# Turned blocks of probabilities and blocks of the values product, one after the other within a slot

## The reference, cut to what matters

```python
s = jnp.einsum('bhqd,bhkd->bhqk', q, k) * scale
s = jnp.where(mask[None, None], s, jnp.finfo(s.dtype).min)
p = jax.nn.softmax(s, axis=-1)
return jnp.einsum('bhqk,bhkd->bhqd', p, v)
...
attn = _causal_attn(q, k, v, SCALE)
lat = _causal_attn(q, lk, lv, SCALE)
return attn @ w_o + lat @ w_lo
```

## Time and profile before

| | us |
|---|---|
| median of 3 runs | 1983.04 (1981.39 to 1983.26) |
| profiled execution | 1982.13 |
| its span, first to last instruction | 1979.6 |
| TensorE busy | 1949.8 (98%) |
| VectorE busy | 1348.5 (68%) |
| GpSimd busy | 1128.6 (57%) |
| ScalarE busy | 1032.7 (52%) |

### The profile page before, as it was taken

How to read it: one execution, slowest core, us unless ns; L and a number is a source line. 1 busy time by engine, 2 the same in 40 slices (tenths; PEclk the granted TensorE clock), 3 DMA queues, 4 the chain that set the end, 5 groups by cost and what they waited for, 6 DMA issues and landing times.

```text
span 1979.6 us, 30315 instructions
## 1 busy us (share of the span) xinstructions
PE 1949.8 (98%) x11104; PEld 1727.1 (87%) x11104; DVE 1348.5 (68%) x3242; ACT 1032.7 (52%) x2335; POOL 1128.6 (57%) x904
## 2 busy tenths in 40 slices
PE   7999999999999999999999999999999999999997
PEld 5989889898898988989898898988989888898985
DVE  5757757576675857757487584766757577575766
ACT  3654627456273653727447273563726547274564
POOL 4647566474754756556475564756546565564750
PEclk8999999999999999999999999999999999999999
DMA  7030120302103030030400203021040300303001
GB/s 265 1 129 3 40 102 12 120 1 101 41 12 120 1 126 16 12 120 1 142 0 27 105 1 141 1 89 43 1 141 1 118 14 18 125 2 116 1 12 43
DMA packets 53074, 117.03 MB, mean 59 GB/s; under 512 B 6848, under 2 KB 8896, under 8 KB 52800
## 3 DMA queue, kind: packets, MB, share of 16 engines
q10 hardware_dynamic: 33936, 69.21, 9.6%
q1 hardware_dynamic: 18992, 45.90, 7.0%
HBM read 108.81 MB, written 6.29 MB: 58 GB/s over the span
## 4 chain that ended last, share of the span: by engine, by line
PE 96%; ACT 2%; DVE 1%; ACTq 1%; POOL 0%; issue 0%; DMA 0%; SPq 0%
PE ps L438 28%; PE ps L440 27%; PE ps L439 27%; PE ps L526 13%; ACT probs L719 1%; ACTq L749 0%; DVE probs L974 0%; ACT acc L794 0%; PE ps L641 0%; PE ps L626 0%; POOL pt_lo L875 0%; ACT k_hi L685 0%; ACT val_hi L685 0%; DMA acc<-xT 0%; DVE stats L1042 0%
## 5 line engine op out<-in xcount | busy, mean ns | idle before, releaser
L903 POOL TENSOR_TENSOR probs<-probs,inv_sum 128x640 f32<-128x640 f32 (+7 forms) x512 | 584.4, 1147 | 383.8 <-DVE inv_sum L981 383.7
L974 DVE CUSTOM_DVE_ANT_0 probs<-ps,mask 128x640 f32<-128x640 f32 (+7 forms) x512 | 383.5, 751 | 68.8 <-PE ps L440 63.4
L719 ACT ACTIVATE probs<-probs,neg_max 128x640 f32<-128x640 f32 (+7 forms) x512 | 398.0, 778 | 52.6 <-DVE neg_max L974 47.5
L915 DVE TENSOR_TENSOR pt_lo<-ps,pt_hi 128x512 fp32r<-128x512 f32 (+3 forms) x512 | 269.2, 549 | 156.5 <-ACT pt_hi L685 156.5
L526 PE MATMUL ps<-ident,probs 128*128 128x128 f32 x2304 | 335.7, 273 | 0.0
L685 ACT ACTIVATE pt_hi<-ps 128x512 fp32r<-128x512 f32 (+3 forms) x512 | 234.3, 489 | 184.2 <-PE ps L526 184.2
L685 ACT ACTIVATE ql_hi<-probs 128x512 fp32r<-128x512 f32 x128 | 81.0, 633 | 439.1 <-POOL probs L894 439.1
L526 PEld LDWEIGHTS ps<-ident,probs 128*128 128x128 f32 x2304 | 274.5, 140 | 27.4
L894 POOL TENSOR_TENSOR probs<-probs 128x512 f32<-128x512 f32 x144 | 186.4, 1295 | 167.6 <-DVE probs L951 167.5
L438 PE MATMUL ps<-val_hi,ql_hi 128*128 128x512 f32 x512 | 205.6, 401 | 0.0
L875 POOL TENSOR_TENSOR pt_lo<-raw,pt_hi 128x1024 fp32r<-128x1024 f32 (+1 forms) x47 | 94.3, 2021 | 191.3 <-ACT pt_hi L685 191.3
(11 more groups left out here) (109 smaller groups left out, 4435.7 us busy)
## 6 DMA issues: line engine op xcount, KB each, us to landing
x_hi<-x_kept ACTq DMA_DIRECT2D x30, 1024.0 KB, 8.8
x_lo<-x_kept ACTq DMA_DIRECT2D x30, 1024.0 KB, 12.2
raw<-wo SPq DMA_DIRECT2D x32, 512.0 KB, 3.6
raw<-wq SPq DMA_DIRECT2D x16, 512.0 KB, 3.9
raw<-wlv SPq DMA_DIRECT2D x16, 512.0 KB, 4.5
raw<-wkv SPq DMA_DIRECT2D x8, 512.0 KB, 7.5
acc<-xT SPq DMA_DIRECT2D x4, 512.0 KB, 6.0
wlk_raw<-wlk SPq DMA_DIRECT2D x16, 128.0 KB, 3.4
```

The costliest lines, as they stand in the source:

```text
L719: nc.scalar.activation(dst, dst, ACT.Exp, bias=neg_max[:, n % 8:n % 8 + 1], scale=-1.0, accum_out=row_sum[:, n % 8:n % 8 + 1]).then_inc(q[ ...
L903: nc.gpsimd.tensor_tensor(b, b, inv_sum[:, k % 8:k % 8 + 1].to_broadcast([P, b.shape[-1]]), ALU.mult).then_inc(q["normed"], 1)
L915: return nc.vector.tensor_tensor(dst, src, h, ALU.subtract)
L974: nc.vector.tensor_tensor_reduce(out=probs_of(n).rearrange("p (b n) -> p b n", b=b), in0=scores_of(n), in1=mask[:, S - w:S].rearrange("p ( ...
```

## The change

In a slot in which a tile is turned and pieces of `PV_AFTER` stand, the pieces are handed to `turn_probs`. It issues one piece (three matmuls, one j) behind each turned block until none is left; pieces that remain follow behind the last block. The signals, the waits and the matmuls themselves are the same, at other places of TensorE's order. The other engines' programs are unchanged.

```diff
-            def turn_probs(g, pair, n):
+            def turn_probs(g, pair, n, between):
+
                 pe.wait_ge(q["normed"], per_pair(g, pair, TILES, n + 1))
...
                     for b in range(b0, b1):
                         mm = pe.transpose(ps[:, T_BANKS[u % len(T_BANKS)], P * (b - b0):P * (b - b0) + P],
                                           probs_of(n)[:, P * b:P * b + P], ident[:])
-                    mm.then_inc(q["turned"], 1)
+                        if b == b1 - 1:
+                            mm.then_inc(q["turned"], 1)
+                        if between:
+                            with_values(g, pair, *between.pop(0))
+                for piece in between:
+                    with_values(g, pair, *piece)
...
+                        pieces = [(m, j, j + 1) for m, j0, j1 in PV_AFTER.get(k, ()) for j in range(j0, j1)]
                         if 0 <= k - T_LAG < TILES:
-                            turn_probs(g, pair, k - T_LAG)
-                        for m, j0, j1 in PV_AFTER.get(k, ()):
-                            with_values(g, pair, m, j0, j1)
+                            turn_probs(g, pair, k - T_LAG, pieces)
+                        else:
+                            for piece in pieces:
+                                with_values(g, pair, *piece)
```

## The result

| | before | after |
|---|---|---|
| median of 6 runs, us | 1982.83 (1981.39 to 1983.90) | 1988.97 (1988.52 to 1991.02) |
| profiled execution, its span | 1982.13, 1979.6 | 1988.90, 1986.2 |

The ratio is 1.0033 with the interval 1.0021 to 1.0045: the change costs 6.1 us. The forecast was 9.6 us, or 1992.6 us in all.

A forecast was written before the change was run, and what follows sets the result against it. TensorE's own list of work was taken to bound the kernel. Extra runs of blocks, 1.9 us, plus the wait of scores(28), 7.7, made 9.6; 1983.04 + 9.6 = 1992.6 us, own range 1989 to 1995 (chance 0.70), wide range 1985 to 1999.

The forecast's parts named there:

- What bounds the kernel: TensorE's own list of work sets the time; hardly a wait to remove, 1.3 us in 8 times on `neg_max`.
- (a): Eight reordered slots: 15 more runs of turned blocks per pair, 0.008 us each over 16 pairs, 1.9 us lost.
- (b): Slot 24's later blocks delay ScalarE and VectorE; new TensorE wait at scores(28), 0.48 us in each of 16 pairs, 7.7 us.
- The sign that was named for it: TensorE's list of waits: `neg_max` with some 24 entries instead of 8, 16 near 0.48 us at scores(28).
- (c): Slots 12, 17, 18, 20, 23, 30, 32: later blocks are covered and cost nothing; uncovered, each 0.1 us would cost 1.6.
- Slot 30's 2.05 us: Slot 30's blocks and tile 30's exponential come 2.05 us later; GpSimd's multiplications still end before tile 30 is turned.
- (d): Slots 12 and 20: pieces arrive sooner, 0.12 and 0.09 us spare after `pt_lo`; cost 0, at worst 4.8 us in all.
- rival 1: Single turned blocks between wide matmuls cost 0.06 instead of 0.11 us, 12.8 us saved: 1978, or 1970 without wait; chance 0.05.
- One premise beside it: Slot 26: two 128-column matmuls start 0.06 us apart, half a turned block's time, so something other than columns bounds a block.

The follow-up runs named there:

- e1: The change in all its slots but slot 24, where both pieces stay behind the six turned blocks; 1981.60 us, ratio 0.9997 to the kernel before.
- e4: The kernel before with only slot 24 reordered: one piece behind the first turned block, the other behind the last; 1984.71 us, ratio 1.0013.
- e6: The whole change, with tile 24's exponential moved behind tile 21's copy on ScalarE and its inverse behind row_max(26) on VectorE; 1983.40 us, ratio 1.0006 to before.
- e7: The kernel before with only slot 24 reordered: its two pieces stand behind the fourth and the fifth turned block; 1986.08 us, ratio 1.0019.
- e2: The kernel before with the change made in slot 24 alone; 1991.39 us, ratio 1.0044.
- e3: The kernel before with both pieces of slot 24 put ahead of its six turned blocks, nothing interleaved; 1992.11 us, ratio 1.0044.
- e5: The kernel before with slot 24 alone reordered as in the change, plus slot 26's 128-column piece brought forward into it; 1995.05 us, ratio 1.0063.

## Why the prediction was right, point by point

**What bounds the kernel.** Right. TensorE had hardly a wait to remove, 1.3 us in 8 times, and the change only added to it.

**(a) More runs.** The mechanism priced here is not there. I took 0.008 us for each of 240 runs, 1.9 us in all; e1 shows 0.002 us for a pair's thirteen together, where the forecast's price makes 0.10. The reading from distances rounded to 0.01 us was below the resolution, and I should have kept its lower bound, 0. This is the term that was mis-sized: 1.9 of the 3.5 us between 9.6 and the measured 6.1. Without it the forecast would have been 7.7 us.

**(b) The wait of scores(28).** Right in place, cause and size: 0.48 forecast, 0.47 in the trace at that point and 0.455 in the pair's length, all sixteen pairs alike. The slack was put together from 0.12 on ScalarE, 0.28 on VectorE and 0.01 on TensorE, 0.41 in sum; e4 measured 0.42. e6 shows the middle of the chain, e7 its first link. The sign that was named for it, entries near 0.48 us in the list of waits, did not appear: the list has 0.2, and the wait shows in the distances alone.

**(c) The covered slots.** Right by e1, in their sum; the times worked out for single queues were not compared one by one. Slot 30's 2.05 us, the largest delay, left no trace on TensorE.

**(d) Earlier pieces.** Right: e1 has both early pieces and no loss, and in slot 20 of after the first piece follows its block without a wait.

```profile
817.14 0.27 PE L527 MATMUL ps<-ident,probs 128*128 128x128 f32 x1
817.16 0.48 PE L438 MATMUL ps<-pt_hi,val_hi 128*128 128x512 f32 x1
817.48 0.39 PE L439 MATMUL ps<-pt_lo,val_hi 128*128 128x512 f32 x1
```

From block to second matmul 0.34 us, less 0.23 for a wide matmul: 0.11 for the single block. The same rows answer rival 1, the hidden load: a block among wide matmuls costs what it costs in a run, not 0.06 us. The rule of the Trainium skill ("TensorE: Matmul & The Clock Gate", "LDWEIGHTS (loading the stationary operand)"), columns over 1.2, gives an estimate of 107 ns for 128 columns of weights and agrees with these 0.11 us as a price for each block; that a wide neighbour hides it was the reading that fell. That the load is what sets the price is not shown.

One premise beside it was read from too little. The 0.06 us between two matmuls of 128 columns in slot 26 is one distance of three:

```profile
829.30 0.27 PE L439 MATMUL ps<-pt_lo,val_hi 128*128 128x128 f32 x1
829.40 0.28 PE L440 MATMUL ps<-pt_hi,val_lo 128*128 128x128 f32 x1
...
829.52 0.84 PE L526 MATMUL ps<-ident,probs 128*128 128x128 f32 x6
```

From 829.24 to 829.52 the three take 0.28 us, 0.09 each. So these rows do not show that a narrow matmul costs half of a turned block. The sum did not use it.

**The sum.** 0.455 x 16 = 7.3 us instead of 9.6, of which (a) explains 1.9 and the size of the wait 0.4. The medians differ by 6.1; the kernel before alone varies by 2.5 us from run to run (1981.39 to 1983.90), and the interval, 4.2 to 8.9 us, holds 7.3. The 1.2 us between the two are within this spread and were not traced further.

## What to carry to other kernels

When the bounding engine has no waits and its instructions cost the same in either order, as the blocks and pieces do here, a new order on it can gain nothing, and its price lies in what it delays elsewhere: take the delayed signal, subtract the slack of each queue it passes, and see what is left where it comes back. Slack is used up first, then delay becomes wait, so later blocks were free in seven slots, even by 2.05 us, while in the eighth 0.885 us cost 0.46 in every pair. Measure such things by the distance between equal instructions of two rounds, to the hundredth, rather than by medians or by the list of waits.

## What was not expected of the hardware

In e2 and e3 the end of the kernel took 2.4 us longer than in the change, though pairs and waits are nearly the same. From the first matmul of the last pair to the last group of matmuls: 1976.00 - 1831.86 = 144.14 us in the change, 1978.89 - 1832.30 = 146.59 in e2. A stretch near the end, in the change and then in e2:

```profile
1965.00:1975.00 10.00, 7.09 (x34) 4.30 (x34) 8.02 (x42) 3.67 (x10) 0.00 (x0) 1.00 0.00 0
```

```profile
1965.00:1975.00 10.00, 7.30 (x21) 4.26 (x22) 6.15 (x28) 3.72 (x10) 0.00 (x0) 0.66 0.00 0
```

The last but two number is the granted clock. In the feed-forward part TensorE is busy for 7 of 10 us, with pauses. In the change it kept the full 2.4 GHz there; in e2 it fell to the lower level, 1.2 GHz, for part of the stretch, 0.66 on average. The same four matmuls behind the same pause show what that costs, again in the change and then in e2:

```profile
1966.18 1.98 PE L649 MATMUL ps<-raw,probs 128*128 128x512 f32 x4 [2.11 <-ACT probs L815]
1968.00 0.38 PE L641 MATMUL ps<-ident,raw 128*128 128x128 f32 x2
```

```profile
1966.63 3.02 PE L652 MATMUL ps<-raw,probs 128*128 128x512 f32 x4 [2.11 <-ACT probs L818]
1969.44 0.63 PE L644 MATMUL ps<-ident,raw 128*128 128x128 f32 x2
```

They take 1.82 us to the next start in the change and 2.81 us in e2. The other profiles agree. If each kernel's own extra per pair is taken off, the last pair and the end take 143.65 us in the kernel before and in e1, 143.69 in the change and 143.70 in e7, where the clock stayed at 1.00 up to the last matmuls. In e4, e5 and e6, whose profiles have about 3.4 us at the lower level, they take 1.3 to 1.6 us more, and in e2 and e3, with about 6.8 us of it, 2.5 more. Why the clock fell near the end in five of the profiles and not in the other four, with the same pause of 2.11 us in the change and in e2, no run here shows.

So two kernels with nearly equal pairs can differ by 2.4 us, 0.12%, through the clock of their last 20 us, and the medians of e2 and e3 hold that as well as the wait. Their single runs fit: with a mean granted clock of 0.995 over the whole run they took 1990.9 to 1992.2 us, and with 0.996 they took 1989.6 to 1990.0.
